# A fixed first adapter, A's rows on ScalarE's DMA queue, and the first two pieces of weights in halves, in a two-layer LoRA kernel

## The reference

```python
def _L1_cond_ref(x, weight, adapter_ids):
    w = weight[adapter_ids]                    # one 1024 x 1024 matrix a sample, of 8
    return jnp.einsum('bsi,boi->bso', x, w)

def _L1_ffn_ref(x, A, B, Wr, br):              # H = 8 experts, rank 16
    router_logits = jnp.einsum('bsd,hd->bsh', x, Wr) + br
    scores = H * jax.nn.softmax(router_logits, axis=-1)
    low = jnp.einsum('bsd,hrd->bshr', x, A)
    return SCALING * jnp.einsum('bshr,hor,bsh->bso', low, B, scores)

x = x + _L0_ffn_ref(_L0_cond_ref(x, L0_cond_weights, itok_B_0_15), L0_ffn_W_base, L0_ffn_b_base, ...)
x = x + _L1_ffn_ref(_L1_cond_ref(x, L1_cond_weight, itok_B_3_7), L1_ffn_A, L1_ffn_B, L1_ffn_Wr, L1_ffn_br)
```

## Time and profile before

| | |
|---|---|
| median of 3 runs | 721.09 us (721.09 to 721.41) |
| profiled execution | 721.44 us |
| its span in the trace, first to last instruction | 719.8 us |
| TensorE busy | 712.7 us, 99% |
| VectorE / ScalarE / GpSimd busy | 401.9 / 116.2 / 58.0 us |
| read from and written to DRAM | 133.24 and 22.35 MB |

### The profile page before, as it was taken

The page is one execution under the profiler, slowest core; times in us unless marked ns, Lnnn a source line. Parts: engine busy times, 40 slices in busy tenths (PEclk is TensorE's granted clock), DMA queues, the critical chain, the costliest instruction groups (busy, mean ns, idle before and its releaser), DMA issues.

```text
span 719.8 us, 12209 instructions
## 1 busy us (share of the span) xinstructions
PE 712.7 (99%) x4454; PEld 640.0 (89%) x4454; DVE 401.9 (56%) x1091; ACT 116.2 (16%) x313; POOL 58.0 (8%) x115
## 2 busy tenths in 40 slices
PE   8999999999999999999999999999999999999997
PEld 8999987898889988898889888988889888999997
DVE  2000298067846576467826784657646782685644
ACT  2222300031103110021003110311002100320112
POOL 1222310001100000001000110000000100010100
PEclk9999999999999999999999999999999999999999
DMA  8999993406755377428724674547742872386552
GB/s 300 410 368 347 389 411 103 173 5 204 252 196 200 120 233 270 170 82 301 278 113 151 212 255 192 193 132 229 261 178 76 298 289 102 147 311 231 197 229 76
DMA packets 38852, 156.26 MB, mean 217 GB/s; under 512 B 8852, under 2 KB 11924, under 8 KB 28564
## 3 DMA queue, kind: packets, MB, share of 16 engines
q1 hardware_dynamic: 27538, 78.66, 29.0%
q0 software_dynamic: 9216, 71.31, 28.7%
q10 hardware_dynamic: 2050, 5.65, 2.0%
HBM read 133.24 MB, written 22.35 MB: 216 GB/s over the span
## 4 chain that ended last, share of the span: by engine, by line
PE 96%; DMA 2%; issue 0%; DVE 0%; SPq 0%; ACT 0%; POOLq 0%; DVEq 0%
PE base_ps L368 18%; PE base_ps L369 18%; PE base_ps L370 18%; PE base_ps L382 10%; PE out_ps L442 4%; PE low_ps L442 4%; PE mix_both L396 4%; PE mix_both L407 3%; PE low_ps L396 2%; PE out_ps L396 2%; PE low_ps L407 2%; PE out_ps L407 2%; PE mix_both L409 1%; PE low_ps L368 1%; PE low_ps L369 1%; PE out_ps L368 1%
## 5 line engine op out<-in xcount | busy, mean ns | idle before, releaser
L368 PE MATMUL base_ps<-yT,w_hi 128*128 128x512 f32 (+1 forms) x576 | 212.2, 368 | 0.7 <-DVE xT L892 0.6
L370 PE MATMUL base_ps<-yT,w_hi 128*128 128x512 f32 (+1 forms) x576 | 211.4, 367 | 0.0
L369 PE MATMUL base_ps<-yT,w_lo 128*128 128x512 f32 (+1 forms) x576 | 211.3, 367 | 0.0
L368 PEld LDWEIGHTS base_ps<-yT,w_hi 128*128 128x128 f32 x576 | 108.5, 188 | 21.0 <-DVE xT L892 2.7
L370 PEld LDWEIGHTS base_ps<-yT,w_hi 128*128 128x128 f32 x576 | 108.5, 188 | 17.9
L369 PEld LDWEIGHTS base_ps<-yT,w_lo 128*128 128x128 f32 x576 | 108.5, 188 | 15.8
L1052 POOL DMA_DIRECT2D adapter<-folded x60 | 32.1, 534 | 554.3 <-PE low_ps L442 481.9
L382 PE MATMUL base_ps<-ag_raw,stage 128*128 128x136 f32 x640 | 75.0, 280 | 0.2 <-DMA stage<-in_w 0.2
L382 PEld LDWEIGHTS base_ps<-ag_raw,stage 128*128 128x128 f32 x640 | 74.8, 191 | 0.4 <-DMA stage<-in_w 0.4
L931 DVE TENSOR_TENSOR xT<-xT,low_ps 128x512 f32<-128x512 f32 (+1 forms) x33 | 21.4, 647 | 90.3 <-PE low_ps L370 90.0
L752 DVE TENSOR_TENSOR yT<-mix_both,yT 128x512 fp32r<-128x512 f32 x32 | 22.0, 691 | 88.3 <-ACT yT L625 88.3
(11 more groups left out here) (189 smaller groups left out, 906.8 us busy)
## 6 DMA issues: line engine op xcount, KB each, us to landing
adapter<-folded POOLq DMA_DIRECT2D x63, 1088.0 KB, 5.3
stage<-in_w SPq DMA_DIRECT2D x39, 512.0 KB, 6.4
x_rows<-in_x SPq DMA_DIRECT2D x32, 512.0 KB, 8.6
xT<-in_x_turned SPq DMA_DIRECT2D x16, 1024.0 KB, 5.7
out<-xT SPq DMA_DIRECT2D x28, 512.0 KB, 2.7
folded<-adapter ACTq DMA_DIRECT2D x10, 544.0 KB, 6.5
w_raw<-in_w SPq DMA_DIRECT2D x8, 256.0 KB, 6.9
w_raw<-in_w SPq DMA_DIRECT2D x4, 512.0 KB, 11.9
```

Of the source, the lines that this page charges most:

```text
L368: pe.matmul(dst, st_hi, mv_lo, start=start, stop=False, skip_group_check=True)
L369: pe.matmul(dst, st_lo, mv_hi, start=False, stop=False, skip_group_check=True)
L370: return pe.matmul(dst, st_hi, mv_hi, start=False, stop=stop, skip_group_check=True)
```

## The change

There are three parts.

1. The first adapter is always number 4 (`FIRST`). SyncE and ScalarE no longer read it from `ids`, and the plan leaves number 4 out in place of sample 0's adapter. If no sample used adapter 4 it would be folded all the same.
2. A's rows move from SyncE's queue to the head of ScalarE's, in two DMAs of half their chunks, with a semaphore for each half. The adapter numbers move there too, behind them. The three small loads that stood there follow.
3. Pieces 0 and 1 of the first adapter come in halves on SyncE's queue, as piece 0 did before, and both halves of a piece have a semaphore. TensorE waits for the second half of piece and rows before its fifth matmul of the piece. The transposes ahead of the fold go from 24 to 10.

```diff
-WARM = 24
+WARM = 10
+
+FIRST = EXPERTS // 2
...
-        ag1_landed = sem("ag1_landed")
-        first_landed = sem("first_landed")
+        ag1_landed = [sem(f"ag1_landed{h}") for h in range(2)]
+
+        first_landed = [sem(f"first_landed{c}") for c in range(2)]
...
-        def first_adapter(eng):
-            eng.wait_ge(ids_landed, 16)
-            return eng.value_load(ids[0:1, SAMPLES:SAMPLES + 1], min_val=0, max_val=EXPERTS - 1)
-
...
-            sp.dma_start(ids[:, SAMPLES:], adapter_ids).then_inc(ids_landed, 16)
-            sp.dma_start(ag1_raw[:, :, :].rearrange("p k n -> p (k n)"), ag1).then_inc(ag1_landed, 16)
-            e = first_adapter(sp)
-
-            piece = w1[bass.ds(KC * e, 1), :, :].rearrange("a p n -> (a p) n")
-            sp.dma_start(stage[:, 0, 0:T], piece[:, 0:T]).then_inc(first_landed, 16)
-            sp.dma_start(stage[:, 0, T:D], piece[:, T:D]).then_inc(unit_landed[0], 16)
-            for c in range(1, KC):
-                load_unit(e, c)
+
+            for c in range(2):
+                sp.dma_start(stage[:, c, 0:T], w1[KC * FIRST + c, :, 0:T]).then_inc(first_landed[c], 16)
+                sp.dma_start(stage[:, c, T:D], w1[KC * FIRST + c, :, T:D]).then_inc(unit_landed[c], 16)
+            for c in range(2, KC):
+                load_unit(FIRST, c)
...
-                    if c == 0 and isinstance(n, int):
-                        pe.wait_ge(first_landed, 16)
+                    in_halves = isinstance(n, int) and c < 2
+                    if in_halves:
+                        pe.wait_ge(first_landed[c], 16)
                     else:
                         pe.wait_ge(unit_landed[c], 16 * n + 16)
                     pe.wait_ge(unit_copied, KC * n + c + 1)
                     for oc in range(KC):
-                        if c == 0 and oc == HALF and isinstance(n, int):
-                            pe.wait_ge(unit_landed[0], 16)
+                        if in_halves and oc == HALF:
+                            pe.wait_ge(unit_landed[c], 16)
+                            pe.wait_ge(ag1_landed[1], 16)
...
-            pe.wait_ge(ag1_landed, 16)
+            pe.wait_ge(ag1_landed[0], 16)
...
+            for h in range(2):
+                chunks = slice(h * HALF, (h + 1) * HALF)
+                act.dma_start(ag1_raw[:, chunks, :].rearrange("p k n -> p (k n)"), ag1[:, h * HALF * HG:(h + 1) * HALF * HG]
+                              ).then_inc(ag1_landed[h], 16)
+            act.dma_start(ids[:, SAMPLES:], adapter_ids).then_inc(ids_landed, 16)
             act.dma_start(ids[:, 0:SAMPLES], cond_ids).then_inc(small_landed, 16)
...
-            e = first_adapter(act)
-            take_adapter(0, e, False)
+            take_adapter(0, FIRST, False)
...
-            plan_after(dve.tensor_scalar(not_first[:, :], expert_no[0:1, :], ids_f[:, 0:1], None,
+            plan_after(dve.tensor_scalar(not_first[:, :], expert_no[0:1, :], float(FIRST), None,
                                          ALU.not_equal), 4)
```

## The result

The changed kernel takes 723.59 us (median of 18 runs, 721.72 to 726.23) where the kernel before takes 721.15 (18 runs, 720.71 to 722.6). The ratio is 1.003, with a 95% interval of 1.0022 to 1.0037: slower by 2.4 us. The prediction said 719.9, in a range of 718.9 to 721.1, and gave slower a chance of 0.10. It was wrong, in size and in sign.

A forecast was written before the change was run, and what follows sets the result against it. The prediction took TensorE to bound the kernel. It summed 1.7 us gained from the fold's start and piece 1's wait, less 0.6 for the bank, to about 1.2 us: 721.09 to 719.9 us, range 718.9 to 721.1.

The forecast's parts named there:

- What bounds the kernel: TensorE, busy 712.7 of 719.8 us, sets the time; what it gains in the first ten microseconds arrives at the end.
- The start of the fold: First fold matmul at 4.8 us instead of 7.33, half pace until 8.0; 1.7 us gained when piece 1 starts.
- Rivals 2 and 3: TensorE's clock rises later, at 10.5 us (720.6 us, 12%), or with the fold, at about 5.5 (718.2, 6%).
- Piece 1 and on: Later pieces on SyncE's queue land 1.0 to 1.5 us earlier; 0 to 0.4 us of TensorE wait, taken as none.
- The banks: Piece 4 waits 0.6 us for ScalarE's first copy, done at 14.3 us, limiting the gain to 1.15 us.
- the landing of that load: ScalarE's last small load, issued at 3.13 us, takes 5.6 us (3.6 to 6.3) and lands at 8.7.
- The sum: 1.7 us from the start and piece 1's wait, less 0.6 for the bank: about 1.2 us gained, median 719.9 us.
- Rival 4: ScalarE's small loads fall behind all of SyncE's pieces and free the bank at 18.7 us: 724.2 us; 10% with other waits.
- The plan: Ready at 10 to 11 us rather than 6.5, SyncE's second-adapter pieces issued from about 12; costed at nothing.
- The range: Median of 718.9 us, just beyond rival 1 (ScalarE in time, 719.4 us, 22%), to 721.1, the gain gone.

The follow-up runs named there:

- e1: The changed kernel with the four wc loads issued one each behind the copies of pieces 4 to 7, no small-load wait before ScalarE's first copy: 720.67 us.
- e5: The changed kernel with 22 transposes of the identity between piece 3 and piece 4: 723.57 us, ratio 1.0029.
- e2: The kernel before with the four wc loads moved behind the copies of pieces 4 to 7: 721.12 us, ratio 0.9996.
- e10: The e3 kernel with 24 transposes ahead of the fold instead of 10: 720.67 us, ratio 0.9985.
- e4: The changed kernel with one more 4 KB load of 128 rows of 32 bytes on ScalarE's queue, which ScalarE also waits for: 725.94 us, ratio 1.007.
- experiment 8: The changed kernel with 22 or 30 transposes between pieces 3 and 4, 723.57 and 723.43 us, and the changed kernel once more, 724.52 us.
- e3: The changed kernel with br_rows and bias_cols issued behind the four wc loads, ScalarE and SyncE waiting for the condition numbers alone: 719.69 us, ratio 0.9982.
- e7: The changed kernel with ScalarE's three small loads issued ahead of A's rows: 725.7 us, ratio 1.0056.
- e8: The kernel before with the first adapter fixed as number 4 and 10 transposes in place of 24: 724.03 us, ratio 1.004.
- e14: The changed kernel itself measured once more, for a second profile: 724.52 us, ratio 1.0038.
- e3b: The kernel before with br_rows and bias_cols behind the wc loads, ScalarE and SyncE waiting for the condition numbers alone: 723.41 us, ratio 1.0025.
- e13: The kernel before with the wc loads behind the copies of pieces 4 to 7, br_rows and bias_cols behind the first adapter: 721.77 us, ratio 1.0003.

## Why the prediction was wrong

*What bounds the kernel.* Right. TensorE sets the time, and what it loses in the fold reaches the end: 2.87 us at 82 us, 2.3 in the span.

*The start of the fold.* Right in size: 4.91 us for the first matmul, predicted 4.8. A's first half landed at 4.9 (0.90 + 4.0), predicted 4.5. The half pace cost part of it, as said, but its end is no fixed time: I took 8.0 us from one profile, and it was 6.1 in the changed kernel's, 8.7 in e1's, 9.3 in e5's, and about 6.0 in e2's, though the start of TensorE was at 2.15 in all. Rivals 2 and 3 therefore were not two ways to go but the spread of one. e10 shows that the start, with all else in order, is worth little beside its 1.65 us.

*Piece 1 and on.* 0.5 us of wait at piece 2, where I had 0 to 0.4.

*The banks.* The mechanism was right, and it decided: the rule "landing of the last small load plus 5.65 us" gives 11.25 + 5.65 = 16.9, and TensorE started piece 4 at 16.95. **The step that failed is the landing of that load**: 5.6 us with an upper bound of 6.3, measured 8.14. I bounded it by the `wc` loads and scaled by the bytes outstanding. A `wc` load is 64 packets; `br_rows` and `bias_cols` are 256, behind each other. On a queue beside a full one the count of packets set the time (e4), 4.5 us for 285. The 6.2 us of the earlier trace rows are another thing: ScalarE's queue moved nothing from 6 to 10 us and 5 packets from 10 to 11, so the first `wc` load, issued at 6.36, mostly waited for its start, and why is open. The bound should have been taken from the pace behind that wait, 73 packets a us: 288 packets behind A's second half, which landed at 6.2 us, give 10.1 by estimate, where I had 8.7. The last few packets moved near 11.

*The sum.* It also left out a term: what TensorE does after a wait. 2.6 us of idling were followed by 2.8 at half pace. I had priced the clock for the start, and not for the wait that I forecast myself at piece 4. As experiment 8 shows, the term is not there in every execution. With the landing at 11.25 and without this term the sum would be 1.4 us of loss, and the measured 2.4 would still have been missed.

*Rival 4* had the right place, the right threshold (slower by 1.44 us if the landing came after 11.3 us; it came at 11.25) and the wrong reason. It had the small loads behind all of SyncE's pieces. They were not held by these: from 6 us on their queue moved 56 to 80 packets in each us, beside SyncE's, and in e3 the condition numbers came through in under 5 us.

*The plan.* It was ready at 10.03 us, and SyncE issued the second adapter's pieces late, but none of TensorE's waits points there. Costing it at nothing was right.

*The range.* It ended at 721.1, and cases that I priced up to 724.2 held a chance of 0.10. As the bound of the landing was too low, so was that chance.

## What to carry to other kernels

Count packets, not only bytes, when a load is put on a queue beside a full one: rows of 32 bytes on 128 partitions are 128 packets, which here moved at 69 to 73 a us and held what was behind them. Issue such loads, if nothing needs them for 100 us, after the rush; here that turned a change that lost 2.4 us into one that gains 1.3. Where an engine issues loads and waits for them ahead of work that frees buffers for another engine, its wait belongs to the chain, even if the profile of before shows that engine idle. And give a wait of TensorE in a stream of matmuls a second price, at half pace, with a chance: here 1.4 us in some executions and nothing in others.

## What the runs showed that I had not expected

Small packets at the head of a queue cost more than behind: e7's A rows took 6.9 and 8.4 us to land behind them, against 4.0 and 4.8 in the changed kernel, and in e8 the whole traffic sank to 125 GB/s for 3 us.

TensorE's clock rose at 6.1 to 9.3 us in executions that began with the same 10 transposes at 2.15 us and did not stand idle for more than 0.9 us after them. By estimate, 3.2 us more at half pace move a kernel's time by up to 1.6 us.

The same wait of TensorE, 2.3 to 2.7 us, was followed by some 3 us at 0.50 in two profiles (after, e14) and by full pace in a third (e3b).

What stays open: in the kernel before with an emptied queue (e13) pieces still landed slowly from 7 to 9 us, and piece 1 was waited for by 0.7 us, without small packets beside it. Why a load on ScalarE's queue moved nothing for some 4 us before its first packet is open too. Why e5's median is 1.0 us above that of the changed kernel's runs whose clock did not fall is not explained. And what decides whether the clock falls after a wait of 2.3 to 2.7 us was not tested.
